# Softmax denominators by GpSimd sums and one product with ones, the shifts by ScalarE, the context by GpSimd's queue

## What is computed

```python
q = heads(x_q @ w_q); k, v = heads(split(x_kv @ w_kv))     # 16 heads of 32, 224 queries, 750 keys
logits = einsum('bhqd,bhkd->bhqk', q, k) * 32 ** -0.5
logits = logits + (arange(Tq)[:, None] - arange(Tk)[None, :]) * w_rel
attn = softmax(logits, axis=-1)
return einsum('bhqk,bhkd->bhqd', attn, v) @ w_proj
```

## Time and profile before

| | |
|---|---|
| median of three runs | 1397.2 us |
| the profiled execution | 1394.94 us |
| its span | 1393.0 us |
| cross-attention, first job to last store | about 342 to 1153 us of the span |
| TensorE busy | 1236.3 us (89%), 10602 instructions |
| VectorE busy | 859.3 us (62%) |
| ScalarE busy | 562.3 us (40%) |
| GpSimd busy | 167.0 us (12%) |
| granted TensorE clock, mean | 0.963 |

### The profile page before, as it was taken

How to read it: one execution, slowest core, us unless ns; L and a number is a source line. 1 busy time by engine, 2 the same in 40 slices (tenths; PEclk the granted TensorE clock), 3 DMA queues, 4 the chain that set the end, 5 groups by cost and what they waited for, 6 DMA issues and landing times. The chain is left out here.

```text
span 1393.0 us, 27044 instructions
## 1 busy us (share of the span) xinstructions
PE 1236.3 (89%) x10602; PEld 953.6 (68%) x10602; DVE 859.3 (62%) x1554; ACT 562.3 (40%) x923; POOL 167.0 (12%) x244
## 2 busy tenths in 40 slices
PE   4799989993799999999999999999999973599997
PEld 3687868882677887787887778777878753344443
DVE  5766646654456566566566565565665545788884
ACT  2222222231234334344343334343343334477775
POOL 0011111114001010110111011011101011001110
PEclk9999999996799999999999999999999995999999
DMA  5222242223234243343243341532432218212211
GB/s 157 86 73 86 75 155 89 84 101 112 68 105 104 48 131 82 72 120 96 62 122 81 96 122 45 134 89 66 113 87 68 65 30 291 114 53 68 62 64 40
DMA packets 69142, 129.52 MB, mean 93 GB/s; under 512 B 12720, under 2 KB 25136, under 8 KB 68512
## 3 DMA queue, kind: packets, MB, share of 16 engines
q1 hardware_dynamic: 65880, 117.19, 29.8%
q0 software_dynamic: 3168, 11.01, 2.3%
HBM read 68.96 MB, written 11.22 MB: 58 GB/s over the span
## 5 line engine op out<-in xcount | busy, mean ns | idle before, releaser
L1146 DVE TENSOR_REDUCE xa_m_part<-xa_psM 112x1 f32<-112x376 f32 x512 | 265.5, 546 | 227.7 <-PE xa_psM L1297 223.7
L1073 ACT ACTIVATE space<-xa_psS 125x448 f32<-125x448 f32 x384 | 207.4, 545 | 251.3 <-PE xa_psS L1281 248.0
L1297 PE MATMUL xa_psM<-xa_k,xa_q 104*112 104x376 f32 x512 | 156.2, 350 | 9.5 <-DVE xa_m_part L1146 6.4
L1281 PE MATMUL xa_psS<-xa_q,xa_k 104*125 104x224 f32 x768 | 144.4, 271 | 0.5 <-ACT space L1073 0.5
L1281 PEld LDWEIGHTS xa_psS<-xa_q,xa_k 104*125 104x125 f32 x768 | 136.7, 187 | 7.4 <-issue 1.1
L1321 PE MATMUL xa_psO<-space,cv 125*32 125x224 f32 x1536 | 110.1, 359 | 1.3 <-ACT space L1073 1.3
L1321 PE MATMUL xa_psO<-space,ones 125*32 125x224 f32 x1536 | 107.8, 352 | 0.0
L1297 PEld LDWEIGHTS xa_psM<-xa_k,xa_q 104*112 104x112 f32 x512 | 88.5, 176 | 27.7 <-DVE xa_m_part L1146 11.1
L1267 PE MATMUL xa_psR<-xa_cT_hi,w_hi 128*128 128x376 f32 x256 | 88.2, 344 | 10.0 <-DVE xa_cT_lo L1136 7.7
L1267 PE MATMUL xa_psR<-xa_cT_hi,w_lo 128*128 128x376 f32 x256 | 90.7, 354 | 0.0
L1267 PE MATMUL xa_psR<-xa_cT_lo,w_hi 128*128 128x376 f32 x256 | 87.7, 343 | 0.0
(11 more groups left out here) (197 smaller groups left out, 2574.3 us busy)
## 6 DMA issues: line engine op xcount, KB each, us to landing
xa_k<-xa_k_st SPq DMA_DIRECT2D x384, 94.0 KB, 2.2
cv<-in_ctx_dram SPq DMA_DIRECT2D x8, 1500.0 KB
xa_q<-xa_q_st SPq DMA_DIRECT2D x192, 56.0 KB, 2.0
cv<-in_L_ffn_w_gate_dram SPq DMA_DIRECT2D x8, 512.0 KB, 4.9
cv<-in_L_ffn_w_up_dram SPq DMA_DIRECT2D x8, 512.0 KB, 6.1
cv<-in_L_ffn_w_down_dram SPq DMA_DIRECT2D x8, 512.0 KB, 6.9
ff_w_raw<-in_L_ffn_w_gate_dram SPq DMA_DIRECT2D x4, 1024.0 KB, 9.1
ff_w_raw<-in_L_ffn_w_up_dram SPq DMA_DIRECT2D x4, 1024.0 KB, 14.1
```

Of the source, the lines that this page charges most:

```text
L1073: nc.scalar.activation(pT[:, (s + i) % 2, j], psS[0:KB, (HG * i + j) % NB, 0:2 * N], ACT.Exp).then_inc(exp_done, 1)
L1146: V.tensor_reduce(m_part[:, seg, t, jj:jj + 1], psM[0:T, seg, 0:SEG], AX.X, ALU.max, negate=True).then_inc(mx_read, 1)
L1281: last = M.matmul(psS[0:KB, (HG * i + j) % NB, a * N:(a + 1) * N], k4[0:ROWS, s % 2, j, col:col + KB], q4[0:ROWS, s, j, :], start=True, st ...
L1297: M.matmul(psM[0:T, seg, 0:SEG], q4[0:ROWS, g, jj, t * T:(t + 1) * T], k4[0:ROWS, g % 2, jj, seg * SEG:(seg + 1) * SEG], start=True, stop= ...
```

## The change

What it does, in five parts.

1. `attend` makes only the products with the values. A new function of GpSimd, `sum_keys`, adds the six key tiles of a slot's exponentials in fp32, five additions of 125 x 896 into a new tile `p_sum`: the first when pair 0 is exponentiated, the next two after pair 1, the last two after pair 2. A new function of TensorE, `denominators`, makes one group of four products of ones with `p_sum`, at beat 2 of the following slot (after the loop for the last one).
2. VectorE's `divide` moves from the end of a slot to beat 2 of the next, and waits for that group. GpSimd's `split_heads` of a slot follows it, ahead of the additions of the next slot. `exponentials` waits for GpSimd to have read the buffer of `pT` that it writes, and GpSimd for `denominators` to have read `p_sum`.
3. ScalarE copies the shifts (`take_shift`), at the same beat.
4. The context loads leave SP's queue for GpSimd's.
5. The start: keys of group 0 come ahead of the turned x, statistics stand behind r3 and normalisation behind r5, and the weight splits stand ahead of K1a and q3.

```diff
@@ attend @@
-                    for col in (0, DEN):
-                        for j in range(HG):
-                            h = HG * s + j
-                            weights = cv[:, b % 2, t, h * HD:(h + 1) * HD] if col == 0 else ones[0:KB, 0:HD]
-                            last = M.matmul(psO[HD * j:HD * (j + 1), col:col + N], weights,
-                                            pT[:, (s + i) % 2, j, a * N:(a + 1) * N], start=t == 0 and col == 0,
-                                            stop=t == NK - 1, skip_group_check=True)
+                    for j in range(HG):
+                        h = HG * s + j
+                        last = M.matmul(psO[HD * j:HD * (j + 1), 0:N], cv[:, b % 2, t, h * HD:(h + 1) * HD],
+                                        pT[:, (s + i) % 2, j, a * N:(a + 1) * N], start=t == 0,
+                                        stop=t == NK - 1, skip_group_check=True)
+            def denominators(b, s):
+                n = NG * b + s
+                pe.wait_ge(p_summed, SUMS * (n + 1))
+                for j in range(HG):
+                    last = M.matmul(psO[HD * j:HD * (j + 1), DEN:DEN + N], ones[0:KB, 0:HD], p_sum[:, j, :],
+                                    start=False, stop=True, skip_group_check=True)
+                last.then_inc(den_full, 1)
@@ TensorE's loop @@
+                        if k == DENOMINATORS_AT and (b, s) != (0, 0):
+                            denominators(*((b, s - 1) if s > 0 else (b - 1, NG - 1)))
                         if part := part_at(b, s, k):
                             do(*part)
+            denominators(B - 1, NG - 1)
@@ gpsimd @@
+            def sum_keys(b, s):
+                n = NG * b + s
+                wait_count(pool, den_full, n)
+                for m in range(SUMS):
+                    i, a = divmod(m + 1, 2)
+                    tile = pT[:, (s + i) % 2, :, a * N:(a + 1) * N]
+                    if m in (0, 1, 3):
+                        wait_apart(pool, exp_done, UNITS * n + HG * (i + 1), pool_passed)
+                    before = pT[:, s % 2, :, 0:N] if m == 0 else p_sum[:]
+                    if m > 0:
+                        pool.wait_ge(p_summed, SUMS * n + m)
+                    nc.gpsimd.tensor_tensor(p_sum[:], before, tile, ALU.add).then_inc(p_summed, 1)
+                pool.wait_ge(p_summed, SUMS * (n + 1))
@@ scalar, exponentials @@
                 if j == 0 and NB * n + i >= 2:
                     act.wait_ge(pv_done, NB * n + i - 1)
+                    act.wait_ge(p_summed, SUMS * n + (-2, 0, 1)[i])
@@ vector @@
-                dve.wait_ge(pv_done, NB * (n + 1))
+                dve.wait_ge(den_full, n + 1)
                 V.reciprocal(den[:], psO[:, DEN:DEN + N]).then_inc(den_ready, 1)
...
-                        if n < NG * B and k == TURN_AT:
-                            take_shift(n)
+                        if k == DENOMINATORS_AT and (b, s) != (0, 0):
+                            divide(*((b, s - 1) if s > 0 else (b - 1, NG - 1)))
...
-                    divide(b, s)
+            divide(B - 1, NG - 1)
@@ the start @@
-    first_fill = ["r0", "r1", "r2", "r3", "r4", "r5", "Xa", "Xb", "K0a", "K0b", "q0", "q1", "K1a", "K1b", "q2", "q3"]
-    SPLIT_AT = {"q0": 2, "K1a": 3}
+    first_fill = ["r0", "r1", "r2", "r3", "r4", "r5", "K0a", "K0b", "Xa", "Xb", "q0", "q1", "K1a", "K1b", "q2", "q3"]
+    SPLIT_AT = {"K1a": 2, "q3": 3}
-                if what == "r1":
+                if what == "r4":
                     statistics(0)
+                if what == "K0a":
                     normalise(0)
```

More of the change, by code:

```diff
@@ L799, in cross_attention @@
     UNITS = NB * HG
+    SUMS = NK - 1
     LAST_STEP = UNITS - HG
@@ L808, in cross_attention @@
     attend_at = {5: 0, 9: 1, 13: 2}
+    DENOMINATORS_AT = 2
     TURN_AT = 12
@@ L880, in cross_attention @@
         m_neg = sb("m_neg", [T, NT, HG])
+        p_sum = sb("p_sum", [KB, HG, N])
         den = sb("den", [P, N])
@@ L901, in cross_attention @@
         st_full, exp_done, pv_done = sem("st_full"), sem("exp_done"), sem("pv_done")
+        p_summed, den_full = sem("p_summed"), sem("den_full")
         mx_full, mx_read, maxima_ready = sem("mx_full"), sem("mx_read"), sem("maxima_ready")
@@ L965, in _ @@
             pack_queries(0, 0)
-            load_context(1)
             pack_keys(0, 1)
@@ L969, in _ @@
             for b in range(B):
-                if b >= 1 and b + 1 < B:
-                    load_context(b + 1)
                 pack_keys(b, 2)
@@ L988, in clear_shift @@
             def clear_shift(b, s):
-                wait_count(pool, oT_ready, NG * b + s)
                 wait_apart(pool, st_full, UNITS * (NG * b + s + 1), pool_passed)
@@ L1011, in split_heads, with load_context @@
                 nc.gpsimd.tensor_tensor(oT_lo[:, s], o_f[:], oT_hi[:, s].bitcast(F32), ALU.subtract).then_inc(oT_ready, 1)
+                pool.wait_ge(oT_ready, n + 1)
+            def sum_keys(b, s):
[11 more added lines that the diff above has]
+                pool.wait_ge(p_summed, SUMS * (n + 1))
+            def load_context(b):
+                wait_count(pool, pv_done, NB * NG * (b - 1))
+                pool.dma_start(cv[:, b % 2], ctx_rows[b].rearrange("(a p) d -> p a d", p=KB)).then_inc(c_in, DMA)
             def store(b):
@@ L1018, in _ @@
             rstd(0)
+            load_context(1)
             rstd(1)
@@ L1021, in _ @@
                 for s in range(NG):
+                    if (b, s) != (0, 0):
+                        split_heads(*((b, s - 1) if s > 0 else (b - 1, NG - 1)))
+                    if s == 0 and b >= 1 and b + 1 < B:
+                        load_context(b + 1)
+                    if s == 1 and b >= 1:
+                        store(b - 1)
+                    if s == 3 and b + 2 < B:
+                        rstd(b + 2)
+                    sum_keys(b, s)
                     if b + 1 < B:
                         clear_shift(b, s)
-                    split_heads(b, s)
-                    if s == 0 and b >= 1:
-                        store(b - 1)
-                    if s == 2 and b + 2 < B:
-                        rstd(b + 2)
+            split_heads(B - 1, NG - 1)
             store(B - 1)
@@ L1066, in take, with take_shift @@
                     copy(cv[:, b % 2, int(what[1])], src[0:KB, :]).then_inc(read[r], 1)
+            def take_shift(n):
+                act.wait_ge(maxima_turned, n + 1)
+                copy(q4[ROW_SHIFT:ROW_SHIFT + HG, n % NG],
+                     psM[0:HG, 0, 0:N].unsqueeze(1).broadcast_to([HG, HG, N])).then_inc(shift_ready, 1)
             def exponentials(b, s, i, j):
@@ L1079, in _ @@
                 take(what, 0)
+            take_shift(0)
             for b in range(B):
@@ L1086, in _ @@
                             exponentials(b, s, *unit)
+                        if k == TURN_AT and NG * b + s + 1 < NG * B:
+                            take_shift(NG * b + s + 1)
         @block.vector
@@ L1183, in _ @@
             join_maxima(0)
-            take_shift(0)
             for b in range(B):
@@ L1258, in do @@
                     if part == 0:
+                        pe.wait_ge(w_split_lo, 2)
                         pe.wait_ge(oT_ready, NG * (b + 1))
@@ L1328, in _ @@
                     do(what, 0, part)
-            pe.wait_ge(w_split_lo, 2)
+            pe.wait_ge(w_split_lo, 1)
             pe.wait_ge(rows_in, ROWS_IN)
```

8 lines of the change are left out of this document (removed).

## The result

The changed kernel takes 1378.5 us (median of 4 runs, 1377.5 to 1380.6) against 1397.8 for the one before on the same chip (4 runs, 1396.3 to 1400.2): a ratio of 0.9861, 95% interval 0.9843 to 0.9879. It is faster by 1.4%. Forecast were 1372.9 us and 1.7%. The profiled execution took 1378.97 us, with a span of 1377.4 against 1393.0, so 15.6 us went between the two profiles, where the sum in the prediction had 24.3.

The account below looks back on a forecast made before the run. TensorE was taken as the bound. Terms -23.2 - 2.3 - 4.5 - 3 + 8.7 = -24.3 us against 1394.94 gave 1370.6, so a median of 1372.9 us was expected; range 1347 to 1397 us.

Parts of the forecast that it names:

- Part 1: TensorE's products, per slot: six groups of ones go (2.3 us), one group comes (0.6 us), net -1.7 us.
- Part 2: VectorE's division at beat 2: half 6 waits for half 4, a new stall of 0.9 us per slot.
- Part 3: GpSimd's additions in the loop: 2.1 us each; the ones group doesn't wait for them, nothing is added.
- Part 4: Rest of the loop: shift copies, later clearing of shift rows, context load issued some 2 us later; each 0.
- Part 5: The start: the 6.40 us wait at r4 goes, first reduction of maxima about 2 us late; -3 us in all.
- Part 6: The end, slots 30 and 31: GpSimd's loop is the longest, 3.7 + 31 + 4.5 = 39.2 us; +8.7 us.
- Rivals A: Beat 4 of each slot: no stall, 26 us more go, 1347 us; chance 0.17.
- B: Slots: VectorE's debt holds half 7 as well, another 0.85 us each, 1397 us, no change; chance 0.10.
- C: Join of the maxima: VectorE held off by a GpSimd addition, 30 us lost, 1403 us; chance 0.09.
- D: GpSimd as the bound: additions at twice the price, 4.2 us, its loop 26 us a slot, 1475 us; chance 0.06.

## Why the prediction came near, and where it was off

- **Part 1** was right in what goes and short in what comes: an attend and its filler's start are 0.89 us apart where the earlier trace rows had 1.65, three times 0.76; the ones group costs 0.71 against the 0.6 taken. Entering it costs 0.09 (0.30 where 0.21 stood), leaving it 0.12 and the slower first product 0.11: so a switch has its cost, which agrees with the drain of which the Trainium skill, "TensorEngine Tiling (Array Packing)", section "Key Properties", speaks, and it is far from the 0.5 us that would have made the sum 12 to 15 us worse.
- **Part 2** named the right place and the right mechanism (half 6 behind half 4 behind the division), and its size was too high: 0.68 instead of 0.9 us. Half 4 had been read 0.2 us sooner after the logits of beat 2 than the sum of durations had it (3.39 us, 3.61 forecast), since the reciprocal and the read of half 4 each start 0.08 us before the end that the row shows for the one ahead; the product, which needs the reciprocal, doesn't. And half 6 would have stood 0.1 later, as the ones group is longer. The division alone, in the old kernel, proves the stall: without the ones group ahead of it 1.35 us a slot. Slots with s=2 gained 0.75 us more than others, where 0.65 stood. Regular slots came out 0.9 us shorter (24.91 to 24.02, 21.98 to 21.07, 23.63 to 22.71), the forecast had 0.8; -2.28 + 0.71 + 0.68 = -0.89 accounts for it, so the shift copy on ScalarE, which was never run by itself, has no cost to hide there.
- **Part 3** was right: 2.11 us an addition, 2.1 taken; no ones group waits in slots 1 to 29; and one addition or five makes no difference there.
- **Part 4** failed, in the term "the context load is issued some 2 us later, wanted 20 us later: 0". The delay was as stated (7.3 us behind the first logits of its slot, 4.9 to 6.2 before), but the cost wasn't with who wants the context. It was with the transfers beside it: the packing of K2 lands with it, and K3a waits. That is 2.9 us over the loop between the two kernels that differ in it alone, and 5.2 from the changed kernel to the better of them (624.3 and 619.1 us from slot 1 to slot 28), in irregular portions.
- **Part 5** failed outright: -3 forecast, +4.1 measured. The wait at r4 did go. What I named as late next (the second load of x, the weight's split) was the smaller part: without the early context load the start takes 57.6 to 58.8 us, where -3 would be 56.6. The term that was missing is the load of the second context. Part 4 prices the loads of the loop, some 2 us later; this one moved from 380.81 to 350.22, 30 us earlier, and stands in no part. It lay beside the K0 packing and made it 6 us late. Two edits that were each priced at little met on the DMA engines.
- **Part 6** was right in kind and 3.6 us short (+12.3 against +8.7). In slot 31 GpSimd's loop took 15.7 us from ones group to ones group (1108.01 to 1123.69), 15.5 reckoned. In slot 30 it took 19.3 (from 1088.67), and that is nearly the whole miss: the sum has five additions in a row, but GpSimd waited 2.96 and 1.20 us for exponentials. Their logits came from a TensorE at the lower clock, and I had priced the chain at the full one. In no kernel with all its additions did the clock stay high there; where it was back at 1.00 for 6.8 us (the kernels with the load behind the second root and with the start as before) the loop took 18.8 and 18.1 us. How much of the 3.8 us is the clock's is open. The first term was 0.8 us too high (2.9 from slot 30's start to the ones group, for 3.7) and the last 0.4 too low (4.9 for 4.5).
- **Slot 29** is in no part. Its join was held by four additions in a row (8.60 us from 1080.01): TensorE waits 1.42 for it where 0.70 was usual, and the slot takes 17.5 us as before the change, where the sum has 0.8 less.
- In the sum the loop's errors cancel, and that is luck (-30.8 against -30.0, by a stall that was too dear, a ones group that was too cheap and loads at nothing); the ends are off by 7.1 and 3.6, and 1.2 us less ahead of cross-attention hide some of it. Rivals A (1347) and B (1397) didn't come: there is a stall, and it is one stall. C's exclusion is real and hidden, and it was no single event in the earlier trace rows either: six of those 16 operations took 1425 to 1515 ns, each beside two GpSimd additions; D's bound is the place that four more additions reach.

## What to carry over

When a change moves a transfer, price it by what else is in flight while it lands, not by when its data is wanted; small transfers that something waits for can be held until a large load beside them has about landed, here some 22 us after its issue. A side engine that is well covered by the loop's fillers can be the bound where the fillers stop; here it paid to leave the last three slots in the old form. And an instruction that waits for nothing can still cost, by what is queued behind it on its own engine.

## What was not expected of the hardware

- In the changed kernel a load of 1500 KB took 21.5 to 24.5 us to land, and packings issued beside it landed at about its end: in the loop ScalarE goes on 0.4 to 1.6 us ahead of the load's landing, at the start 2.1 us behind it (374.28 and 372.1). The last transfer of the packing needed 7.8 us beside the load and 1.7 without.
- The clock: around the start of slot 30 of the changed kernel TensorE was busy 3.43 and 3.15 of 5 us in the two windows ahead of the fall, in the kernel before 4.30 and 3.04, and there the clock stayed at 1.00. With one addition a slot it was 4.16 and 3.08, and then 0.66 for one window of 5 us. Once low, it stayed low for 41 us in the changed kernel; in two others with the same end it came back for 6.8 us in between. What decides between these isn't shown here.
- VectorE's join of 112x8 took 167 ns alone and up to 1182 beside an addition on GpSimd; the additions kept 2.07 to 2.18 us in that kernel.
